# A two-layer graph network on one core: 49 edge groups for 50, source indices first, interleaved gathers and dense work, and a wait at every third indirect transfer

## The reference, cut to what matters

```python
# layer 0
feat = concatenate([x[dst], x[src] - x[dst]])
messages = relu(feat @ W1 + b1) @ W2 + b2
x = layernorm(x + segment_max(messages, dst))     # 0 for a row with no edge
# layer 1
h = x + segment_sum(x[src], dst)
h = relu(h @ W1 + b1) @ W2 + b2
x = layernorm(x + (x @ Wres + bres) + h)
```

## Time and profile before

| | |
|---|---|
| median of 3 runs | 1454.56 us (1453.96 to 1475.86) |
| profiled execution, own time | 1442.36 us |
| its span, first to last instruction | 1440.5 us |
| busy: PE, DVE | 1176.8 us (82%), 1085.9 us (75%) |
| busy: POOL, ACT | 833.3 us (58%), 818.3 us (57%) |
| mean granted PE clock | 0.957 of 2.4 GHz |

### The profile page before, as it was taken

How to read it: one execution, slowest core, us unless ns; L and a number is a source line. 1 busy time by engine, 2 the same in 40 slices (tenths; PEclk the granted TensorE clock), 3 DMA queues, 4 the chain that set the end, 5 groups by cost and what they waited for, 6 DMA issues and landing times. The chain is left out here.

```text
span 1440.5 us, 32925 instructions
## 1 busy us (share of the span) xinstructions
PE 1176.8 (82%) x7573; PEld 862.2 (60%) x7573; DVE 1085.9 (75%) x5525; ACT 818.3 (57%) x2320; POOL 833.3 (58%) x812
## 2 busy tenths in 40 slices
PE   3899999972277777777669998999899999999992
PEld 1667777651133334334357877887776777777771
DVE  6698999862177777777748897897787888888881
ACT  1355555541155555555426665665657777777772
POOL 2666666666666666665066666666655555555513
PEclk9899999987599999999879999999999999999996
DMA  3666666643256655556445565655655555556541
GB/s 96 179 193 195 204 199 196 194 130 94 53 175 175 171 176 168 169 172 156 122 123 177 173 194 160 193 182 165 177 177 152 175 180 184 182 188 187 180 142 50
DMA packets 162414, 236.11 MB, mean 164 GB/s; under 512 B 27296, under 2 KB 70526, under 8 KB 162369
## 3 DMA queue, kind: packets, MB, share of 16 engines
q1 hardware_dynamic: 135184, 195.53, 42.8%
q0 software_dynamic: 25600, 39.60, 11.3%
q10 hardware_dynamic: 1584, 0.53, 0.1%
HBM read 131.05 MB, written 90.91 MB: 154 GB/s over the span
## 5 line engine op out<-in xcount | busy, mean ns | idle before, releaser
L576 POOL DMA_INDIRECT out<-edge_rows,idx x200 | 201.7, 1008 | 190.7 <-issue 127.7
L1221 PE MATMUL psY<-wcr,xT 128*128 128x128 f32 x1568 | 305.3, 276 | 0.0
L1220 PE MATMUL psY<-wc,hT 128*128 128x128 f32 x1568 | 304.8, 276 | 0.5 <-issue 0.5
L569 POOL DMA_INDIRECT edge_rows<-x1e_table,idx x200 | 206.1, 1031 | 151.2 <-issue 96.9
L569 POOL DMA_INDIRECT edge_rows<-in_x,idx x200 | 214.0, 1070 | 134.4 <-issue 64.8
L569 POOL DMA_INDIRECT xd_rows<-in_x,idx x200 | 209.2, 1046 | 120.6 <-issue 63.9
L1220 PEld LDWEIGHTS psY<-wc,hT 128*128 128x128 f32 x1568 | 256.2, 194 | 7.3 <-issue 0.8
L1072 ACT ACTIVATE o_rows<-psY,rs_b 128x128 f32<-128x128 f32 x784 | 223.6, 368 | 56.0 <-issue 40.3
L1221 PEld LDWEIGHTS psY<-wcr,xT 128*128 128x128 f32 x1568 | 240.0, 193 | 0.0
L1231 PE MATMUL psH<-xT,wc 128*128 128x512 f32 x392 | 212.9, 625 | 16.7 <-issue 9.7
L1052 ACT ACTIVATE sd_a<-mv_a,eps_col 128x4 f32<-128x4 f32 x196 | 58.4, 298 | 274.4 <-issue 150.5
(11 more groups left out here) (131 smaller groups left out, 2132.2 us busy)
## 6 DMA issues: line engine op xcount, KB each, us to landing
x_in<-in_x SPq DMA_DIRECT2D x196, 256.0 KB
out<-o_rows SPq DMA_DIRECT2D x196, 256.0 KB
xs_rows<-edge_rows SPq DMA_DIRECT2D x100, 256.0 KB
xs_rows<-src_dram SPq DMA_DIRECT2D x50, 256.0 KB
mask<-mask_dram SPq DMA_DIRECT2D x100, 128.0 KB
x1e_table<-shared SPq DMA_DIRECT2D x50, 256.0 KB
x1eT_spill<-x1eT SPq DMA_DIRECT2D x50, 256.0 KB
x1eT<-x1eT_spill SPq DMA_DIRECT2D x50, 256.0 KB
```

The lines of the kernel that those rows point to most:

```text
L569: nc.gpsimd.indirect_dma_start(to, None, table, bass.IndirectOffsetOnAxis(idx[:, what, t:t + 1], 0), bounds_check=rows - 1, oob_is_err=err ...
L576: nc.gpsimd.indirect_dma_start(table, bass.IndirectOffsetOnAxis(idx[:, SCAT, t:t + 1], 0), frm, None, bounds_check=N - 1, oob_is_err=False ...
L1220: t_.matmul(to[:, cut(t)], h[:, cut(t)], wc2[:, :], start=False, stop=False, skip_group_check=True)
L1221: last = t_.matmul(to[:, cut(t)], xt[:, cut(t)], wcr[:, :], start=False, stop=t == TILES - 1, skip_group_check=True)
```

## The change

There are 49 groups, a stage A in octets of eight steps with a body of four dense units in them (one before every other step), six octets in all, so that stage C has 17 bodies for 23. Stage B has 49 steps, 48 of them with a dense unit as before. The source indices are loaded, turned and handed to POOL before the weights and the other indices are prepared. The last 11 `gather_src` are issued between the `gather_dst` of stage A, one after every fourth. The count for a scatter is read ahead, before the last tile of the group before. POOL waits for its own completion after every third indirect transfer.

```diff
-    GROUPS = 2 * -(-E // (2 * ROWS))
+    GROUPS = -(-E // ROWS)
+    OF_PARITY = [len(range(q, GROUPS, 2)) for q in range(2)]
+    OCTETS = GROUPS // (2 * SLOTS)
+    FIRST_A = 1 + QUADS
+    FIRST_B = FIRST_A + OCTETS
+    SRC_FIRST = GROUPS - 11
...
+            def octet_a(i, b):
+                for r in range(2 * SLOTS):
+                    j = i * 2 + r // SLOTS
+                    if r % 2 == 0:
+                        dense(b, r // 2)
+                    step_a(j, r % SLOTS)
...
-            with eng.Fori(1, QUADS - 1) as j:
-                quad_a(j)
-            quad_a(QUADS - 1)
-            step_a(QUADS, 0)
+            with eng.Fori(1, OCTETS - 1) as i:
+                octet_a(i, i + FIRST_A)
+            octet_a(OCTETS - 1, OCTETS - 1 + FIRST_A)
+            for r in range(SLOTS):
+                step_a(QUADS - 1, r)
...
+            sp.wait_ge(s_iz, 1)
+            load_indices(0, src, s_is)
             for k in range(3):
                 load(0, k)
-
-            sp.wait_ge(s_iz, 1)
...
+            sp.wait_ge(s_iz, 2)
+            for n in (1, 2):
+                load_indices(n, dst, s_i)
...
-            pool.wait_ge(s_dv, IDX_STEP)
+            pool.wait_ge(s_dv, SRC_IDX_STEP)
...
-                if issued[0] % 2 == 0:
+                if issued[0] % 3 == 0:
                     kw["engine_sem"] = s_issued
 
-            def issued_pair():
-                if issued[0] % 2 == 0:
-                    pool.wait_ge(s_issued, issued[0] // 2)
+            def issued_three():
+                if issued[0] % 3 == 0:
+                    pool.wait_ge(s_issued, issued[0] // 3)
...
-            for g in range(GROUPS):
+            for g in range(SRC_FIRST):
                 gather_src(g)
                 if g == GROUPS // 2:
+                    pool.wait_ge(s_dv, IDX_STEP)
                     for d in range(SLOTS):
                         gather_dst(d)
+            late = SRC_FIRST
             for g in range(SLOTS, GROUPS):
                 gather_dst(g)
+                if g % 4 == 0 and late < GROUPS:
+                    gather_src(late)
+                    late += 1
...
+            count = stores_needed(0)
             for g in range(GROUPS):
                 j, r = divmod(g, SLOTS)
                 wait(pool, final[r], 16 * TILES * j)
                 pool.wait_ge(res_done, g + 1)
                 if g < WHOLE:
-                    before = pool.value_load(stores_16[0:1, g:g + 1], min_val=0, max_val=16 * LAST)
-                    count = pool.snap(before + 16)
...
                 for t in range(TILES):
+                    if t == TILES - 1 and g + 1 < WHOLE:
+                        count = stores_needed(g + 1)
                     scatter(out, edge_rows[:, cut(g * TILES + t)], g * TILES + t, final[r])
...
+            dve.wait_ge(s_is, 16 * 3)
+            link(v.tensor_copy(idx_f[:, 0, :, :], idx_in[:, 0, :, :]))
             norm1_stats(0, 0)
             norm1_ready(0, 0)
             norm1_var(0, 0)
+            dve.wait_ge(s_pe, 1)
+            link(v.tensor_copy(idx[:, 0, :], psE[0][:, 0:2 * P]))
+            assert step[0] == SRC_IDX_STEP
...
+            pe.wait_ge(s_dv, 1)
+            for h in range(2):
+                last = t_.transpose(psE[0][:, cut(h)], idx_f[:, 0, h, :], ident[:, :])
+            last.then_inc(s_pe, 1)
```

More of the change, by code:

```diff
@@ L179, in gnn_program @@
         s_i = sem("indices_loaded")
+        s_is = sem("src_indices_loaded")
         s_iz = sem("index_pads_written")
@@ L260, in gnn_program @@
         final = sems("final", SLOTS)
-        WEIGHT_STEPS = 15
+        SRC_IDX_STEP = 2
+        WEIGHT_STEPS = SRC_IDX_STEP + 15
         SRC_STEP = WEIGHT_STEPS + 2
@@ L313, in quad_s @@
                     step_s(j, r, b)
-            def quad_a(j):
-                for r in range(SLOTS):
-                    step_a(j, r)
+            def octet_a(i, b):
[4 more added lines that the diff above has]
+                    step_a(j, r % SLOTS)
             def quad_b(j, b):
@@ L325, in walk @@
             quad_s(0, 1)
-            with eng.Fori(1, QUADS - 1) as j:
+            with eng.Fori(1, QUADS - 2) as j:
                 quad_s(j, j + 1)
-            quad_s(QUADS - 1, QUADS)
+            for j in (QUADS - 2, QUADS - 1):
+                quad_s(j, j + 1)
             lead_a()
-            quad_a(0)
-            with eng.Fori(1, QUADS - 1) as j:
-                quad_a(j)
-            quad_a(QUADS - 1)
-            step_a(QUADS, 0)
+            octet_a(0, FIRST_A)
+            with eng.Fori(1, OCTETS - 1) as i:
[3 more added lines that the diff above has]
+                step_a(QUADS - 1, r)
             lead_b()
             quad_b(0, FIRST_B)
-            with eng.Fori(1, QUADS - 1) as j:
+            with eng.Fori(1, QUADS - 2) as j:
                 quad_b(j, j + FIRST_B)
+            quad_b(QUADS - 2, QUADS - 2 + FIRST_B)
             quad_b(QUADS - 1, None)
@@ L496, in step_b, with load_indices @@
                 feed_b(j, r + 1)
+            HALF = P * P
+            def load_indices(n, a, done):
+                sp.dma_start(idx_in[:, n, 0, :], a[0:HALF].rearrange("(j p) -> j p", p=P)).then_inc(done, 16)
+                sp.dma_start(idx_in[0:FULL - P, n, 1, :],
+                             a[HALF:FULL * P].rearrange("(j p) -> j p", p=P)).then_inc(done, 16)
+                sp.dma_start(idx_in[FULL - P:FULL - P + 1, n, 1, 0:REST],
+                             a[FULL * P:E].rearrange("(j p) -> j p", j=1)).then_inc(done, 16)
+            sp.wait_ge(s_iz, 1)
+            load_indices(0, src, s_is)
             for k in range(3):
                 load(0, k)
-            sp.wait_ge(s_iz, 1)
[L502 to L508, removed]
+            sp.wait_ge(s_iz, 2)
+            for n in (1, 2):
+                load_indices(n, dst, s_i)
             sp.dma_start(idx_in[:, 3, 0, :], dst[1:HALF + 1].rearrange("(j p) -> j p", p=P)).then_inc(s_i, 16)
@@ L1000, in _ @@
             assert step[0] == MASK_STEP
[L1001 to L1004 removed]
+            dve.wait_ge(s_pe, 4)
+            v.tensor_copy(idx[:, 1, :], psE[1][:, 0:2 * P])
+            link(v.tensor_copy(idx[:, 2, :], psE[1][:, 2 * P:4 * P]))
             assert step[0] == IDX_STEP
@@ L1201, in _ @@
             pe.wait_ge(s_dv, SCAT_STEP)
-            for n in range(3):
+            for n in range(2):
                 for h in range(2):
-                    at = 2 * n + h
-                    last = t_.transpose(psE[at // 4][:, cut(at % 4)], idx_f[:, n, h, :], ident[:, :])
+                    last = t_.transpose(psE[1][:, cut(2 * n + h)], idx_f[:, 1 + n, h, :], ident[:, :])
             last.then_inc(s_pe, 1)
```

39 lines of the change are left out of this document (19 added, 20 removed).

## The result

The changed kernel takes 1689.86 us (median of 4 runs, 1675.96 to 1719.43) beside 1460.53 us for the kernel before (4 runs, 1453.96 to 1475.86): ratio 1.150, 95% interval 1.137 to 1.163. The forecast was 1385 us. The profiled execution has 1675.96 us and a span of 1674.0 us.

The account below looks back on a forecast made before the run. Bound by stage: POOL up to 387, a waiting chain in A, PE in C, dense stores at the end. Span 1440.5 - 51.3 - 13.9 + 2.9 - 6.2 = 1372.0, plus 1.9, scaled by 1.0085: 1385 us, range 1350 to 1420.

Parts of the forecast that it names:

- Stage S keeps its dense units: Stage S: one group less removes only some edge work beside the dense units; counted 0, ends 0 and -5.
- The third-transfer wait: POOL in stage A: ten transfers fit into two steps of 17.5 us even in pairs (15.7), so nothing gained.
- The hole: Before stage A: source indices first and 11 late source groups remove PE's wait for `xd_rows`, -51.3 us.
- The dense unit in stage A: Stage A: each of 24 units costs 3.6 us, +86.4 us, against -83.5 us in stage C; together +2.9 us.
- rival 3: Stage A: dense unit loads come too late, 7.7 us a unit, 98 us more, time 1484; chance 0.05.
- Stage C and the tail: End: dense stores set it, last at 1357, POOL 9 us early; four scatters for eight behind it, -6.2 us.
- POOL's own numbers: POOL: gaps 0.3, 0.3, 0.8 in threes; first groups end nearer 268; 196 gathers of `x1e_table` take 297 us.
- Rival 1: Stage A: dense units fill its waits, 2.1 us a unit, 36 us less, time 1349; chance 0.15.
- Rival 2: POOL: third transfer in flight costs what the wait saved, time 1420, or 1442 without the count's gain; chance 0.14.
- The port rule: DVE's two-port mode locks POOL out, stretching its transfers: scatter group 12.7 us, kernel some 1670 us; chance 0.01.

Follow-up runs that it names:

- e1: The changed kernel with POOL's wait after every second indirect transfer instead of every third: 1419.76 us, ratio 0.990 to the kernel before.
- e6: e1 with no dense unit in stage A and 5 late source groups for 11: 1367.48 us, ratio 0.952 to the kernel before.
- e9: The changed kernel with source and destination gathers of `x` skipping every row but row 0, constants in their place: 1807.03 us beside 1455.84 for the kernel before.
- e7: The kernel before with the wait at every third transfer and stage A's loop written out: 1617.04 us beside 1437.94 for the kernel before.
- e8: The kernel before with stage A's loop written out, the wait at every second transfer as before: 1441.6 us.
- e17: The changed kernel with waits after every fourth transfer and a 128x1280 memset on POOL behind each wait: 1454.1 us, ratio 1.013 to the kernel before.
- e12: The changed kernel with waits at every second transfer and a small memset on POOL behind each: 1438.24 us, ratio 0.989 to the kernel before.
- e3: The changed kernel with POOL's wait after every indirect transfer: 1546.64 us, ratio 1.078 to the kernel before.
- e16: The changed kernel, waits after every third transfer, with a 128x1280 memset on POOL behind each wait: 1463.0 us, ratio 1.019 to the kernel before.

## Why the prediction was wrong

**The step that failed** is the one that is not in the sum: "Stage S keeps its dense units and loses only some edge work beside them; I count 0", and "The third-transfer wait is worth nothing here". The new pace was weighed only for what it does to POOL. Its price on the other engines was put at nothing without a reason; the earlier trace rows show only what the wait costs POOL, a gap of 0.81 us for 0.31. Measured, it is 255.5 us of span (the changed kernel against e1), some 230 us by the ratios, and with it away 1418.5 us of span are left for the 1372.0 forecast. That the number in `pace` does it is shown from both sides; how it reaches the other engines is not (below).

**The hole.** Right: PE's wait of 51.28 is gone in e1 and in the changed kernel, where it waits for no `xd_rows` at all. POOL stands before `gather_dst(4)` as forecast; the 40 us became 115.81 in the changed kernel, since stage S ended later, and 19.58 in e1.

**The dense unit in stage A** was mis-sized. Pairs of steps take 18.4 us in e1 (49 scans in 442.0 us, 9.21 each), 4.5 over 2 x 6.96, for the 3.6 of the sum: +22 us. In the changed kernel it is 5.2. The load that rival 3 named takes part: in stage A DVE waits 39.1 us for `x_in` (39.6 in e1), 1.6 for each of the 24 units, where the sum had 1 us, mostly hidden, and rival 3 had 4.73. How much of the 22 us this wait makes no run tells. One such step of the changed kernel:

```profile
488.24 0.49 DVE L691 BATCH_NORM_STATS2 bn_a<-x_in 128x6 f32<-128x128 f32 x2 [2.63 <-DMA x_in<-in_x]
...
492.94 0.20 DVE L850 RECIPROCAL rs_e<-sd_e 128x8 f32<-128x8 f32 x1 [1.43 <-ACT sd_e L1084]
```

So the interleaving costs more than it takes out of stage C: 24 x 4.5 = 108 against 83.5 us. e6, without it, has 53.8 us less of span than e1. Read by stages, S is 4.2 us shorter there, A 92.8, B 12.8, and the stretch behind B 56.0 longer, where the 24 units put back would make 83.5. The 27.5 us between are POOL: it was late at the end in e1, as the next paragraph shows, and in e6 its last two scatter groups wait 20.73 and 6.44 us for stores. In A e6 does not reach 6.96 us a step, since 44 source groups stand before the destination rows of group 4 and PE waits 19.6 us in all for `xd_rows`. Why B is shorter no run shows.

**Stage C and the tail.** Right: 272.2 us from the last scan of B on, 272 forecast, and POOL early:

```profile
854.25 1.01 POOL L586 DMA_INDIRECT edge_rows<-x1e_table,idx  x1 [42.01 <-DMA x1e_table<-shared]
...
1659.56 0.98 POOL L593 DMA_INDIRECT out<-edge_rows,idx  x1 [6.71 <-DMA out<-o_rows]
```

The last scatter group waits 6.71 us for a store. But POOL was early because the others were late. In pairs (e1) it was late, as the prediction had it for pairs (some 20 us): 296.3 us from the last scan of B on, 24 more than 272. No scatter of its last groups waits for a store; a group of e1 begins like this:

```profile
1397.84 0.98 POOL L593 DMA_INDIRECT out<-edge_rows,idx  x1 [1.08 <-issue]
```

With the dense unit's 22 us that makes 1372.0 + 22 + 24 = 1418, e1's span. Luck is in how well it closes: the first scan of A comes 7 us sooner than forecast and stage B takes 7 us more.

**POOL's own numbers.** Right: gaps of 0.30, 0.30 and about 0.81 us, no transfer beyond 1.552 us, its 42 first groups done at 265 (268 forecast) and its 196 gathers of `x1e_table` in 294.4 us from first to last start (297 forecast).

**The rivals.** Rival 1 is out (9.2 us a step of A in e1). Rival 2 gave an upper end of 1442 through POOL's own time, and neither of its signs came (a second gap over 0.5 us, a last group that waits for no store); the price was paid by the others. Rival 3's sign came, DVE waiting for `x_in` in stage A, but at a third of its size; that the kernel got slower, as rival 3 alone of the three had it, was luck. The port rule, given 1 in 100, named some 1670 us, close to the time that came, but not by what came: it stretches POOL's transfers, and none was stretched; in the changed kernel it is PE, DVE and ACT that start late. The same section of the Trainium skill (SBUF — State Buffer, "Who interferes with whom") says that PE and ACT wait for nobody at these ports, so it has no place for a PE that does 49 instructions in 120 us.

**What stays open** is the resource. What the runs exclude: the bytes gathered and the time of the DMA engines (e9), that stage A's loop is what spares it (e7, e8), the length of a run as such (e17), and for pairs POOL's busy share (e12). What is left is argued, not shown: something that each indirect transfer takes from the fetching or the starting of instructions on the other engines, be it by the writing on POOL or by its packets and completions. That the gaps read "issue" and "remote" speaks for it. No run measures it directly. Every execution here carries a span and a clock of its own from the profiler, so the runs can't tell either whether its recording takes part.

## What to carry to other kernels

A wait on an engine that looks idle may be what keeps the others running: before one is taken away, bound not only what its engine gains but what its higher rate costs everybody else, and try it alone. Indirect transfers of 128 rows on POOL should here be kept at 1.6 us or more apart on average over a stretch; waits after every second do it, and a pause of 1.4 us after four nearly does (1.013 for 0.990). In a profile, the mark is many small "issue" gaps on PE and "remote" ones on DVE in exactly those stretches in which POOL issues without waiting, with the DMA engines less busy than elsewhere.

## What the runs showed of the hardware that was not expected

- Transfers on POOL 1.52 us apart for 1.67 took PE from 948 to 563 instructions in 120 us; 1.31 us apart, with almost no data moved, they left 49. POOL's own durations and gaps show nothing of it.
- Even at 1.68 us there is a price: with 1.88 (e3) PE was 120.00 of 120 us busy and a step of S took 4.53 us, where e1, the same code in pairs on the same chip, had 113.81 us and 4.90.
- A memset on POOL behind a wait for its own transfer adds nothing to the gap up to about 0.5 us (it stays 0.8); one of 1.2 to 1.5 us after every third transfer drew a DVE operation from 498 to 968 ns (e16), after every fourth to 528 (e17).
- The stalls cost clock as well: with PE 91.17 of 120 us busy 0.79 of 2.4 GHz was granted over 100 to 220 us, where the kernel before, 114.23 us busy, had 1.00.
